# The next tile's x split ahead of the gating, in the first tile of a fused state-space and gated-MLP kernel

## The reference

```
x = x + L0(x, length)      # causal convolution along 512 with a kernel made from 64 complex modes, masked by length
x = x + L1(x, index)       # gated MLP with low-rank adapters picked per batch
gate = x @ W_gate.T + adapter(A_gate, B_gate);  up = x @ W_up.T + adapter(A_up, B_up)
act  = silu(gate) * up                           # 1376 wide
down = act @ W_down.T + adapter(A_down, B_down)
```

## Time and profile before

| what | value |
|---|---|
| median of 3 runs | 540.23 us (539.28 to 541.24) |
| the profiled execution | 540.83 us |
| its span, first to last instruction | 538.8 us |
| PE busy | 494.6 us (92%) |
| DVE busy | 243.8 us (45%) |
| ACT busy | 153.1 us (28%) |
| mean granted TensorE clock | 0.987 |

### The profile page before, as it was taken

One profiled execution on the slowest core, in us unless ns is written; L12 is line 12 of the kernel. 1 busy time (PEld: TensorE's weight loads), 2 busy tenths in 40 slices (PEclk: granted clock), 3 DMA queues, 4 the chain that ended last, 5 costly groups with the idle time before them and its releaser, 6 DMA issues.

```text
span 538.8 us, 9538 instructions
## 1 busy us (share of the span) xinstructions
PE 494.6 (92%) x3036; PEld 443.0 (82%) x3036; DVE 243.8 (45%) x489; ACT 153.1 (28%) x283; POOL 38.8 (7%) x55
## 2 busy tenths in 40 slices
PE   0098798599999999999999999999999999999997
PEld 0087697588898989898988889898989898989896
DVE  7883164454343535353535344444435353534423
ACT  5781002422322222222322231322222222222221
POOL 1006700000000000000000000000000000000000
PEclk9999799989999999999999999999999999999999
DMA  7899995274748484949474747475757665665601
GB/s 261 301 328 375 297 325 155 40 156 97 149 105 153 116 152 117 152 116 154 112 155 118 154 113 153 118 143 119 140 127 140 127 139 133 131 143 112 151 31 39
DMA packets 182614, 82.79 MB, mean 154 GB/s; under 512 B 128034, under 2 KB 165474, under 8 KB 182594
## 3 DMA queue, kind: packets, MB, share of 16 engines
q1 hardware_dynamic: 182594, 82.54, 64.0%
HBM read 63.46 MB, written 19.04 MB: 153 GB/s over the span
## 4 chain that ended last, share of the span: by engine, by line
PE 84%; DMA 5%; DVE 5%; SPq 3%; issue 1%; ACT 0%; DVEq 0%; ACTq 0%
PE ps_g L1113 16%; PE ps_u L1113 16%; PE ps_da L1045 13%; PE ps_db L1045 12%; PE ps_x L1113 11%; PE ps_g L1081 5%; PE ps_g L1008 3%; DMA toep<-kpad 3%; PE ps_x L1037 2%; DMA kpad<-k_sb 2%; PE ps_u L1008 2%; PE ps_u L1045 2%; PE ps_x L1081 1%; PE ps_da L1072 1%; SPq L366 1%
## 5 line engine op out<-in xcount | busy, mean ns | idle before, releaser
L886 DVE TENSOR_TENSOR ht_lo<-h_raw,ht_hi 128x512 fp32r<-128x512 f32 (+1 forms) x45 | 27.1, 603 | 92.0 <-ACT ht_hi L537 80.7
L537 ACT CAST ht_hi<-h_raw 128x512 fp32r<-128x512 f32 (+1 forms) x45 | 24.7, 549 | 154.7 <-DMA h_raw<-hrow 150.3
L1113 PE MATMUL ps_g<-w_hi,x_hi 128*128 128x512 f32 x128 | 51.8, 405 | 7.2 <-DVE x_lo L843 5.8
L907 DVE TENSOR_TENSOR h_act<-h_act,ps_u 128x512 f32<-128x512 f32 x32 | 22.0, 688 | 73.5 <-ACT h_act L572 73.5
L1113 PE MATMUL ps_u<-w_hi,x_hi 128*128 128x512 f32 x128 | 51.7, 404 | 0.0
L1113 PE MATMUL ps_g<-w_lo,x_hi 128*128 128x512 f32 x128 | 51.5, 402 | 0.0
L1113 PE MATMUL ps_g<-w_hi,x_lo 128*128 128x512 f32 x128 | 51.4, 402 | 0.0
L1113 PE MATMUL ps_u<-w_hi,x_lo 128*128 128x512 f32 x128 | 50.6, 396 | 0.0
L1113 PE MATMUL ps_u<-w_lo,x_hi 128*128 128x512 f32 x128 | 50.5, 395 | 0.0
L1045 PE MATMUL ps_da<-wd_hi,ht_hi 128*128 128x288 f32 (+1 forms) x165 | 50.4, 306 | 0.0
L1045 PE MATMUL ps_db<-wd_hi,ht_lo 128*128 128x288 f32 (+1 forms) x165 | 48.7, 295 | 0.0
(11 more groups left out here) (214 smaller groups left out, 1073.1 us busy)
## 6 DMA issues: line engine op xcount, KB each, us to landing
b_raw<-btab SPq DMA_DIRECT2D x128, 86.0 KB, 2.8
toep<-kpad SPq DMA_DIRECT2D x16, 512.0 KB, 7.5
h_raw<-hrow SPq DMA_DIRECT2D x30, 256.0 KB, 3.2
ad_raw<-dtab SPq DMA_DIRECT2D x64, 88.0 KB, 2.4
um<-xr SPq DMA_DIRECT2D x16, 256.0 KB, 5.4
x<-xT SPq DMA_DIRECT2D x8, 512.0 KB, 7.7
w_raw<-wgu SPq DMA_DIRECT2D x8, 512.0 KB, 10.5
a_raw<-atab SPq DMA_DIRECT2D x64, 64.0 KB, 1.9
```

The lines of the kernel that those rows point to most:

```text
L537: nc.scalar.copy(ht_hi[:, f0:f0 + full, :], raw[:, 0:full, :]).then_inc(hthi_ok, 1)
L886: V.tensor_tensor(ht_lo[:, f0:f0 + full, :], raw[:, 0:full, :], ht_hi[:, f0:f0 + full, :].bitcast(F32), ALU.subtract).then_inc(htlo_ok, 1)
L907: V.tensor_tensor(h_act[:, 0:w], h_act[:, 0:w], ps_up[c][:, 0:w], ALU.mult).then_inc(act_ok, 1)
L1113: T.matmul(ps[:, 0:w], xs[:, kb, :], ws[:, kb, col:col + w], start=(kb == 0 and xs is x_hi and ws is w_hi), stop=False)
```

## The change

In tile 0 (k == 0), ScalarE makes x_hi of tile 1 before the three silus instead of after them, and VectorE makes x_lo of tile 1 before the three gatings instead of after them. In all other tiles the order stays. Nothing is added or removed.

```
@@ ScalarE, body @@
                 act.wait_ge(tm_ok, t + 1)
                 nc.scalar.copy(t_hi[:, :], t_m[:, :, :].rearrange("p h b -> p (h b)")).then_inc(thi_ok, 1)
+                if k == 0:
+                    x_hi_part(t + 1)
                 for c in range(NC):
                     silu(c)
                     if last:
                         turned_hi_part(c)
-                if not last:
+                if k > 0 and not last:
                     x_hi_part(t + 1)
                 if k == 0:
                     for n in range(NP_GU + 3, NP_GU + 6):
@@ VectorE, body @@
                 V.tensor_tensor(t_lo[:, :], t_m[:, :, :].rearrange("p h b -> p (h b)"), t_hi[:, :].bitcast(F32),
                                 ALU.subtract).then_inc(tlo_ok, 1)
+                if k == 0:
+                    x_lo_part(t + 1)
                 for c in range(NC):
                     gated(c)
                     if last:
                         ht_lo_part(t, c, True)
                     else:
                         square_h(c)
-                if not last:
+                if k > 0 and not last:
                     x_lo_part(t + 1)
                 if k == 0:
                     for n in range(NP_GU + 3, NP_GU + 6):
```

## The result

The changed kernel took 543.9 us (median of 8, 541.91 to 545.46) against 539.4 us for the kernel before in the same session (538.03 to 541.61): ratio 1.0073, 95% interval 1.0045 to 1.0101. It is slower, by 3.9 us at the ratio. The profiled execution took 545.1 us with a span of 543.1.

The account below looks back on a forecast made before the run. The round trip from tile 0's first silu through SP's queue to t_m of tile 1 was taken to bound the kernel. First silu 1.92 plus clock 2.5 gave 4.4 us on 540.23: 544.6 us, range 542.0 to 546.2.

Parts of the forecast that it names:

- Parts 1 and 2: ScalarE, end of tile 0: x_hi cast and uncovered Silu table load delay the first silu, 1.92 us together.
- Rival D: ScalarE: uncovered table switch also drains, first silu 3.3 us late, 5.8 us slower in all, 546.0 us; chance 0.04.
- A: ScalarE: table load stays hidden behind t_hi, 3.1 us slower, 543.4 us; chance 0.06.
- Parts 3 and 4: VectorE's x_lo is hidden; TensorE starts tile 1 at 103.4, gaining 3.7 us, all ending before its t_m wait at 117.5.
- Part 5: First silu to t_m of tile 1 keeps its length; TensorE goes on at 126.25 after waiting 8.6 us.
- Part 6: TensorE's clock falls in the 8.6 us wait ahead of base(2, 1), costing 2.5 us.
- rival B: TensorE's clock does not fall, or the round trip shrinks as much: 1.9 us slower, 542.2 us; chance 0.08.
- Rival C: TensorE's start of tile 1 sets the end, t_m ready by 117.5: 6.7 us faster, 533.5 us; chance 0.04.

Follow-up runs that it names:

- hi_only: Kernel before with only ScalarE's half of the change: x_hi of tile 1 ahead of the silus, x_lo left behind the gating; ratio 1.0044 to before.
- preload: Changed kernel plus a silu of one column ahead of x_hi in ScalarE's idle time, drawing the table load forward; ratio 1.0047 to the kernel before.
- slots: Kernel before with x_hi and x_lo of tile 1 moved behind chunk 0 of the gating; ratio 1.0029 to before.
- tm_only: Kernel before with t_m, t_hi and t_lo of tile 1 ahead of the last chunk's split, x split unmoved; ratio 0.9984 to before.
- slots_warm: Kernel before with tile 1's x split behind chunk 0 of the gating, plus 28 unused matmuls ahead of the wait for t_m; ratio 1.0018 to before.
- number 10: Kernel before with x split behind gating chunk 0, t_m early in tile 1 and all later tiles, tile 1's b split ahead of the second chunk's; ratio 0.9975.
- number 11: Kernel before with t_m early in tile 1 and later tiles and tile 1's b split early, x split left behind all gatings; ratio 1.0061 to before.
- best: Kernel before with early x split, t_m and b, plus tile 2's adapter table load moved into tile 0's body; 533.65 us against 540.63, ratio 0.9870.
- warm: Changed kernel plus 30 unused matmuls in tile 1 ahead of the wait for t_m; ratio 1.0037 to the kernel before.
- preload_warm: Changed kernel plus an early one-column silu and 30 unused matmuls ahead of tile 1's wait for t_m; ratio 1.0026 to the kernel before.

## Why the prediction was right, point by point

It said 544.6 us, slower by 4.4 us. Measured were 543.9 and 4.5 by the medians, 3.9 by the ratio, and 4.07 in the head. The median of the kernel before was 540.23 in its three runs and 539.4 in these eight, so that 544.6 starts 0.8 us high.

- **Parts 1 and 2, the chain of the first silu: 1.92 us.** From the first MLP matmul to the first silu it took 100.08 - 82.97 = 17.11 us before and 102.25 - 83.15 = 19.10 after: 1.99. `hi_only` shows that it reaches the end, `preload` that 1.35 to 1.4 of it is the load.
- **The rule on table loads.** By the Trainium skill (ScalarE: Activation LUTs, What ACT_TABLE_LOAD costs) a drain of 1.38 us comes with a switch. The trace disagrees: in the changed kernel, where nothing covers it, the activation starts at 102.25, 1.30 us after the load began at 100.95, which is the load alone. Rival D is out, and so is A.
- **Parts 3 and 4.** TensorE was to start at 103.4 (in fact 103.71, of which 0.18 is the later start of the MLP) with a wait of 2.2 us (2.31), and to arrive at 117.5 (117.96).
- **Part 5, the round trip keeps its length.** Roughly. From first silu to t_m it took 23.92 us before and 24.37 after, 0.45 more. One issue in the group of b_raw is the difference in kind; the chain that ended last in the changed kernel shows it (start, us, what), where its neighbours take 0.34:

```profile
111.50 0.34 SPq L321
...
112.05 1.70 SPq L321
...
122.97 2.45 DMA h_raw<-hrow
```

  That group took 5.60 us against 4.24, while ad_raw took 2.04 against 2.88, so the net is 0.5. `hi_only` again has 23.92. What makes single issues long was not tried, so the prediction's "keeps its length" was off by 0.45 us for a reason that stays open.
- **Part 6, the clock: 2.5 us.** The mechanism held, the size was over: 1.62 in the changed kernel. `preload` lost 129.84 - 123.74 - 4.20 = 1.90 and `slots` 2.52. These three waits were 9.0, 8.7 and 6.6 us long, so the cost doesn't grow with the wait. How soon the clock comes back differs from one execution to the next: after waits of 5.84 us (before) and 5.85 us (`tm_only`) the first 12 matmuls took 5.23 and 4.21 us. The 2.5 was taken from one such execution. The errors, +0.07, +0.45 and -0.88 us, cancel in part: that the sum of 4.4 came within 0.4 us of the head's 4.07 is in that part luck. Of rival B only that much was true.
- **Rival C, faster,** needed t_m by 117.5; it came at 126.62. `slots` and `slots_warm` show that no early start pays while this is so. That it pays once t_m, b and tile 2's table are out of the way is shown in part: number 10 with the early split is 4.6 us faster than number 11 without it, and `best`, which has all, 7 us faster than before; `best` without the split was not run.
- From tile 2 on all is as before: lora_a to lora_a 27.57 us, no wait until the last 0.7.

The 0.5 to 0.7 us between head and all in `preload`, `warm` and `preload_warm` lie for the most part in one tile each, the one with a wait for its own t_m: 0.40 us at 208.99, 0.30 at 511.53 and 0.55 at 180.67. What makes t_m late there stays open.

## What to carry to other kernels

An engine's longest wait shows where it stands, not what holds the end back: ask the chain that ended last whether the wait is on it, and what the engine runs into if that wait goes. Here one wait became 3.5 us shorter and the next 8.3 us longer, at a place where the fall of TensorE's clock had nothing to hide behind, and the work moved ahead stood in front of the real chain. Operations that are hidden, such as a table load, are hidden by a particular wait; count them again when anything is put between. When the true chain is loosened, follow it through the next tiles until it holds: here the early start alone cost time, t_m alone and t_m, b and the early start together brought under 0.3%, and with the early load on top it was 7 us.

## What the runs showed of the hardware

- The load of an activation table (1.28 us) runs ahead of the waits of its own activation but not of those of an operation ahead of it: hidden at 95.98 before, at 100.95 after.
- After waits of 6.6 to 9.0 us in TensorE the return to the full clock cost between 1.6 and 2.5 us, in no order with the length. After one of 1.8 us in number 10 the granted clock fell as well (0.80 over 134 to 142 us), and the stretch was 1.8 us longer beyond the wait; after the 2.3 us in the changed kernel it stayed at 1.00 (103 to 109 us). 28 or 30 unused matmuls in the wait kept it at 1.00.
- The same kind of DMA issue on SP's queue mostly takes 0.32 to 0.36 us, and now and then 1.2 to 1.7.
